# Cross-attention kernel: the loads of key-major probabilities move from SP's DMA queue to ScalarE's own

## The reference

```python
a = layer_norm(ctx, gamma, beta)
Q, K, V = x @ Wq.T, a @ Wk.T, a @ Wv.T            # split in 16 heads of 64
scores = where(mask, Q K^T * 64 ** -0.5, -inf)     # 1024 x 64 for each head
out = softmax(scores) V                            # heads joined: 1024 x 1024
return x + tanh(gate) * (out @ Wo.T)
```

## Time and profile before

| | us |
|---|---|
| median of 3 runs | 1524.88 (1522.81 to 1528.76) |
| the profiled execution | 1520.95 |
| its span, first to last instruction | 1519.2 |
| TensorE busy | 1478.4 |
| VectorE busy | 1146.3 |
| ScalarE busy | 893.7 |
| GpSimd busy | 525.2 |

### The profile page before, as it was taken

One profiled execution on the slowest core, in us unless ns is written; L12 is line 12 of the kernel. 1 busy time (PEld: TensorE's weight loads), 2 busy tenths in 40 slices (PEclk: granted clock), 3 DMA queues, 4 the chain that ended last, 5 costly groups with the idle time before them and its releaser, 6 DMA issues.

```text
span 1519.2 us, 20234 instructions
## 1 busy us (share of the span) xinstructions
PE 1478.4 (97%) x6624; PEld 1194.7 (79%) x6624; DVE 1146.3 (75%) x1349; ACT 893.7 (59%) x1894; POOL 525.2 (35%) x364
## 2 busy tenths in 40 slices
PE   6999999999999999999999999999999999999999
PEld 5666788788888788888787788877778787787887
DVE  6345788687878787878866787878878787777843
ACT  4456645454545455546675776766667666666721
POOL 5334000000000000000123675666766566766741
PEclk9999999999999999999999999999999999999999
DMA  7699865566565656565489887777887887888842
GB/s 272 208 384 390 295 219 182 200 208 214 193 215 191 218 180 229 180 208 175 145 270 337 259 254 237 239 226 230 241 258 238 228 248 212 238 250 244 246 145 72
DMA packets 305736, 348.52 MB, mean 229 GB/s; under 512 B 37216, under 2 KB 178656, under 8 KB 305632
## 3 DMA queue, kind: packets, MB, share of 16 engines
q1 hardware_dynamic: 305632, 347.23, 71.7%
HBM read 198.26 MB, written 145.75 MB: 226 GB/s over the span
## 4 chain that ended last, share of the span: by engine, by line
PE 57%; DMA 12%; SPq 10%; issue 7%; DVE 6%; POOL 5%; ACT 4%; DVEq 0%; ACTq 0%; POOLq 0%
PE banks L1169 18%; PE banks L1170 17%; PE banks L1171 17%; DMA p_by_key<-p_scratch 4%; SPq L469 4%; PE banks L1198 3%; POOL p_parts L650 3%; DMA out<-c_out 3%; SPq L489 2%; DMA probs<-s_scratch 2%; DVE a_ring L955 2%; ACT probs L799 2%; POOL probs L644 1%; DVE parts L961 1%; DMA wo_split_scratch<-wo_ring 1%
## 5 line engine op out<-in xcount | busy, mean ns | idle before, releaser
L1169 PE MATMUL banks<-parts,a_ring 128*128 128x512 f32 x1792 | 701.7, 392 | 12.0 <-DVE a_ring L955 11.3
L1171 PE MATMUL banks<-parts,a_ring 128*128 128x512 f32 x1792 | 698.1, 390 | 0.0
L1170 PE MATMUL banks<-parts,a_ring 128*128 128x512 f32 x1792 | 698.0, 390 | 0.0
L1169 PEld LDWEIGHTS banks<-parts,a_ring 128*128 128x128 f32 x1792 | 336.7, 188 | 89.1 <-DVE a_ring L955 18.3
L1171 PEld LDWEIGHTS banks<-parts,a_ring 128*128 128x128 f32 x1792 | 336.7, 188 | 70.9
L1170 PEld LDWEIGHTS banks<-parts,a_ring 128*128 128x128 f32 x1792 | 336.9, 188 | 68.9
L799 ACT ACTIVATE probs<-probs,neg_max 128x64 f32<-128x64 f32 x1024 | 258.7, 337 | 1.7 <-DVE neg_max L1061 1.7
L1047 DVE TENSOR_TENSOR c_out<-banks,c_out 128x1024 f32<-128x1024 f32 x159 | 192.7, 1212 | 85.7 <-PE banks L1171 59.5
L650 POOL TENSOR_TENSOR p_parts<-p_by_key,p_parts 128x512 fp32r<-128x512 f32 x112 | 163.0, 1456 | 213.2 <-ACT p_parts L808 213.0
L955 DVE TENSOR_TENSOR a_ring<-a_sum,a_ring 128x1024 fp32r<-128x1024 f32 x128 | 185.6, 1450 | 66.7 <-ACT a_ring L735 66.3
L735 ACT CAST a_ring<-a_sum 128x1024 fp32r<-128x1024 f32 x128 | 134.3, 1050 | 164.8 <-PE banks L1171 132.7
(11 more groups left out here) (76 smaller groups left out, 1309.6 us busy)
## 6 DMA issues: line engine op xcount, KB each, us to landing
xq<-x_t SPq DMA_DIRECT2D x32, 1024.0 KB, 6.5
s_scratch<-c_out SPq DMA_DIRECT2D x64, 512.0 KB, 3.1
probs<-s_scratch SPq DMA_DIRECT2D x128, 256.0 KB, 3.8
c_out<-x SPq DMA_DIRECT2D x64, 512.0 KB, 5.0
out<-c_out SPq DMA_DIRECT2D x63, 512.0 KB, 4.7
b_raw<-m_scratch SPq DMA_DIRECT2D x29, 1024.0 KB, 6.7
m_scratch<-m_stage SPq DMA_DIRECT2D x16, 1792.0 KB, 13.9
p_scratch<-p_turned SPq DMA_DIRECT2D x448, 64.0 KB, 2.6
```

The lines of the kernel that those rows point to most:

```text
L1169: pe.matmul(to, wl, mh, start=first, stop=False, skip_group_check=joined)
L1170: pe.matmul(to, wh, ml, start=False, stop=False, skip_group_check=joined)
L1171: return pe.matmul(to, wh, mh, start=False, stop=last, skip_group_check=joined)
```

## The change

`fetch_p` leaves SP's program and stands in ScalarE's, with the same waits, the same source, destination and semaphore. It is called in the same slot, z = `soft_slot` + 8, three slots before the unit's rounding, and there ahead of the slot's roundings, copies and exponentials. All DMAs before were issued by SP; these 112 are now issued by ScalarE. Nothing else is changed.

```diff
-            def fetch_p(u):                      # in SP's program
-                v = u - ON_PE
-                if v == 0:
-                    sp.wait_ge(mask_made, ROUNDS)
-                elif v == 1:
-                    sp.wait_ge(b_lo_made, 14 * B)
-                elif v >= BY_KEY:
-                    sp.wait_ge(p_lo_made, u - BY_KEY + 1)
-                sp.wait_ge(p_stored[v % TURNED], 64 * (v // TURNED + 1))
-                sp.dma_start(by_key(u), p_scr[v].rearrange("p i n -> p (i n)")).then_inc(p_in[v % BY_KEY], 16)
...
-                for u in units(soft_slot, z - FETCH):
-                    if u >= ON_PE:
-                        fetch_p(u)
...
+            def fetch_p(u):                      # in ScalarE's program
+                v = u - ON_PE
+                if v == 0:
+                    act.wait_ge(mask_made, ROUNDS)
+                elif v == 1:
+                    act.wait_ge(b_lo_made, 14 * B)
+                elif v >= BY_KEY:
+                    act.wait_ge(p_lo_made, u - BY_KEY + 1)
+                act.wait_ge(p_stored[v % TURNED], 64 * (v // TURNED + 1))
+                nc.scalar.dma_start(by_key(u), p_scr[v].rearrange("p i n -> p (i n)")).then_inc(p_in[v % BY_KEY], 16)
...
                 for z in (2 * s, 2 * s + 1):
+                    for u in units(soft_slot, z - FETCH):
+                        if u >= ON_PE:
+                            fetch_p(u)
                     for u in units(split_slot, z):
                         split_p_hi(u)
```

## The result

The changed kernel takes **1548.65 us** (median of 4 runs, 1542.68 to 1550.01) against 1523.99 before: ratio 1.0156, 95% interval 1.0126 to 1.0186. It is slower by 24.7 us. The profiled execution took 1542.68 us with a span of 1540.9. The first part of the kernel is the same; the time is lost between the first and the last load of `p_by_key`, which are 645.7 us apart (827.4 to 1473.1) where they were 620.4 apart.

The account below looks back on a forecast made before the run. ScalarE, without slack, was taken to make TensorE late. Its 420.1 us busy + 33 issues + 189 new wait = 642 against 618.5 gave +24 on 1520.95: 1545 us, with an 8-in-10 range of 1508 to 1580.

Parts of the forecast that it names:

- The new wait: ScalarE's wait at the load's new place for its unit's store to land: 2.46 - 0.77 = 1.69 us a unit, 189 us.
- The unrelieved wait: Store's landing minus ScalarE's arrival at the load's new place, with SP as late as before: mean 2.46 us over 96 units.
- The relief: Stores leave SP earlier once loads are gone from its unbroken runs of issues: mean 0.77 us a unit off the wait.
- ScalarE's sum: ScalarE's time in the stretch: 420.1 busy + 33 issues + 189 new wait = 642 us, against 618.5 filled before.
- The issues: 112 load issues added to ScalarE's queue, 0.295 us each: 33 us, with bounds of nothing and 125 us.
- SP isn't the bound on average: SP's two largest waits in the stretch, 63.8 and 57.2 us, leave its issues counting only in crowded runs.
- TensorE's bound: TensorE busy 605.7 of the stretch's 620 us, so at most 14.3 us can be won.
- the first rival: SP's lag goes, stores start at VectorE's turn's end, mean wait falls below 1.36 us: 1507 to 1514 us; chance 0.24.
- ScalarE has no slack left: ScalarE's busy time and waits fill 618.5 of the stretch's 620 us, so a wait in its queue makes TensorE late.
- break-even: New wait at which ScalarE's time equals the stretch's 620 us: 1.49 us a unit.
- The ring: Rival: loop through ScalarE, VectorE's turn and SP's store closes, 14 rounds each losing another 3 us: 1587 us; chance 0.07.
- The landing: Store lands 2.6 us after issue begins, 2.15 after its group's end; loads take 3.3 us; their own queue speeds none.

## Why the prediction was right, point by point

*The time*: 1545 forecast, 1548.65 measured; +24 on the profiled execution forecast, +21.7 between the two profiled executions. The mechanism is the forecast one: ScalarE's wait for a load became a wait for the load's store (the run with the wait alone costs as much as the whole change and more), and it is longer. That the number came so close is in part luck, as the next points show.

*The new wait*: 1.69 us a unit. In the trace after, ScalarE's idle time between the row ahead of a load and the load's issue sums to 187 us over the 112 loads, 1.67 us each. The agreement is better than the terms behind it. The unrelieved wait was too high at 2.46 us: with SP burdened again by the small DMAs the same reading gives 1.98, and with the loads left on SP and only the wait moved it is 1.94. The relief was too high as well: 0.77 us against 1.98 - 1.67 = 0.31. The two errors cancelled. What failed is that both were read against ScalarE's arrival in the *old* run, which each wait changes; units 34 and 35 show it, and no run counts it for the rest. Nor is 2.46 firm as a reading of the kernel before: the same 96 units give 2.54 us by the prediction's rule for the landing (the group's end plus 2.15 us), and 2.68 by the landings on record, further still from what came.

*ScalarE's sum*: 642 us forecast. The rows after give 420.9 busy and 221 of waits (113.4 + 81.6 + 17.1 + 2.8 and smaller ones), 642; but busy time and waits fill any engine's stretch, here 641 us, so only the parts can be compared. The waits for stores, with the issues that they hold, are 212 us, where 189 + 33 were forecast. The other waits, taken to vanish from 20 us, stand at 9.

*The issues*: 33 us of ScalarE's time forecast, 0.295 us each. The issue is shorter than was taken (0.326 us against 0.395), and 112 longer ones (0.498 us) cost 6 us of the kernel's time where they were tried alone. The 33 us come near for the wrong place of the load alone: there 31 of the 37 us of issuing fall into time in which no instruction of ScalarE runs. Without the wait the prediction's lower bound holds, an issue beside a running instruction, for nothing.

*"SP isn't the bound on average"*: wrong. 121 us of waits in the stretch were taken for slack. With the loads left on SP, each of 112 issues more costs 0.34 us of the kernel's time, and 112 fewer bring it to TensorE's bound. That SP waits because what it waits for is late too, in part through SP, is my reading; no run parts it. The prediction named this only in the first rival.

*"ScalarE has no slack left"*: true after the change, not enough before it. SP's load one slot earlier took 111 us off ScalarE's wait for loads (178.4 to 67.5) and nothing off the time. The time fell in the runs that took issues off SP and left ScalarE a short wait at the load's place or none.

*The first rival, faster by SP's relief*: its mechanism is real, and its condition was the deciding one: a mean wait below 1.36 us at the new place. At three slots it isn't met (1.67, and even with 112 fewer issues on SP it is 1.47, just under the prediction's break-even of 1.49; the ratio is then 1.0013). At two slots (0.88) and one (0.02) it is met, and there the gain appears. That gain still needs SP's relief: with 112 small DMAs given back to SP, the mean wait at one slot stays low (0.1) and the ratio is 1.0079.

*TensorE's bound, "14.3 us is all that can be won"*: too small. A matmul's row is 0.39 us long, while the next begins 0.227 us after it, so a stall of up to 0.16 us leaves no idle time and each longer one shows 0.16 us too little. Summed from start to start (every step over 0.26 us, less 0.227), TensorE's stalls are 20.7 us before and 38.7 after. The load one slot ahead of its rounding won 20.0 us and left 0.8 us of stalls; V's loads left out won 18.5 and left none. The idle time of 38 us that was forecast, against 14, is one by busy time, and by that measure it came out as 24.8; that 38.7 by starts is near it is chance.

*The ring*: not at three slots, but at four (ratio 1.1416).

*The landing*: stores 2.5 us from their issue, where 2.6 were read. A unit's last store lands 1.94 us after the end of its group in the median, where 2.15 was taken. Loads take 3.8 instead of 3.3 us; at three slots ScalarE doesn't wait for one of them. The rule cited from the Trainium skill ("DMA: Bandwidth & Descriptors", "Issuing engines are not separate DMA queues") fits: the own queue made no landing shorter. The section adds that the issuing time saved is usually small relative to the DMA itself. So it is here, 0.395 us against 3.3 from issue to landing; yet 112 issues off SP are worth more than 1% of the kernel's time.

## What to carry to other kernels

A load moved to the consumer's queue brings its own wait along, for the data to be there; try it later than the old queue had it (one slot ahead instead of three turned +1.6% into -1.3% here). One slot, about 3.2 us, is even less than issue and landing together (0.33 + 3.8 us); the short wait for the load that this leaves, 0.7 us a unit, cost less than the wait for its store. The issue itself is nearly free on a compute engine's queue while that engine has an instruction running, and adds to the wait where the engine has run dry. Read the wait at the new place unit by unit from the trace before, and carry each wait on to the arrival at the next place. A DMA queue that waits in total can still be the bound: test it with a few issues more and fewer before calling it slack.

## What the runs showed that was not expected

- The same small DMA costs the kernel 0.34 us on SP's queue (38 us for 112) and 0.05 us on ScalarE's (6 us for 112).
- The issue of the same 256 KB load takes 0.326 us on ScalarE, with little spread (0.325 to 0.391), and 0.395 on SP (0.343 to 1.122). The small DMA shows no such difference (0.498 on ScalarE, 0.497 on SP). Why isn't settled.
- ScalarE's queue can issue a DMA beside the instruction that stands ahead of it, and even before that one begins: the load of unit 8 in the changed kernel starts at 874.04, the high half ahead of it in the program (L721) at 874.23. So it is for 14 of the 112 loads.
- The price of the load's place is steep and one-sided: 1.142, 1.016, 0.990, 0.987 for four, three, two and one slots ahead of the rounding.
- A wait with no releaser in the view ("issue") need not be free of cause: here those of VectorE at `c_out` each end 0.08 us after a load of `c_out` has landed.
